# GroupNorm and attention on one core: scalar operands for GpSimd's high parts, and a new order of its list

## The chip, the core and the metric

The kernel runs on one core of a Trainium2 chip. The metric is the device time of one execution in microseconds (us). The profiler records one execution; its span runs from the first to the last recorded instruction. Engines are named as in the profile: PE is TensorE's matmuls and PEld its weight loads, DVE is VectorE, ACT is ScalarE, POOL is GpSimd, SP is SyncE, which here only issues transfers.

## The reference

Eight images `x[b]` of 128 channels by 1024 positions (32 by 32) go through a GroupNorm of 32 groups, a single-head self-attention over the positions, and a residual sum:

```python
h = group_norm(x, gn_w, gn_b)                       # 32 groups of 4 channels
q = einsum('bcn,oc->bno', h, wq) + bq
k = einsum('bcn,oc->bon', h, wk) + bk
v = einsum('bcn,oc->bno', h, wv) + bv
alpha = softmax(q @ k / sqrt(128))                  # 1024 x 1024 for each image
out = einsum('bnc,oc->bon', alpha @ v, wo) + bo
return out + x
```

## The kernel before

The weights are folded once: `wu` stands for wq and wk together, `wvc` for wv and wo together with one column more. For an image (a "batch" `b`, 0 to 7) the kernel makes `h` from x with a scale `ga` and an offset `gc` per channel, `u` from h (what the logits take instead of q), and `v` from h, whose last column gives the bias `c_tok` of each row of logits. To keep float32 accuracy on float16 matmuls, every operand is split in a high part (the value rounded to float16) and a low part (value minus high part), and each product is three matmuls.

The 1024 rows of logits of a batch are 8 tiles of 128. For tile `n`: PE makes the logits in one of three PSUM buffers `S` (lines 537 to 541, `logits`), DVE adds `c_tok` and takes the row extreme (L855, `row_max`), ACT makes the exponentials (L722) and the float16 high part (L733), DVE the low part (L871), SP issues a DMA that transposes both (L234), and PE multiplies by v nine tiles later (`values`, L564 to L566, `LAG = 9`), four tiles at a time into one PSUM bank `O`. All five engines have a list written out by hand, and wait on semaphores. PE's list per batch is: logits of tile n; behind tile 0 the second half of u (`project_u(b, 1)`); behind tiles 1 and 2 the last two parts of v (`project_v`); behind 3 and 5 the first half of u and the first part of v of the next batch; behind 4 and 6 two small matmuls for the statistics of batch b+2; and after each of these one quarter of `values`.

ACT copies u and v out of PSUM to float32 tiles in SBUF (`copy_u` L688, `copy_v` L698) and the products to `av` (`copy_values`, L707). POOL, which cannot reach PSUM, then makes in a round `b` of its list:

- `group_affine(b+1)` (L309 to L318): four instructions of one column that give ga and gc. It waits for the standard deviation.
- `h_parts(b+1, half)`: h (L330), its high part (L333) and its low part (L336), 512 columns each. Half 0 waits until all logits of batch b-1 are done, because the buffer is shared.
- `u_parts(b, 1)` and `u_parts(b+1, 0)`: high and low part of u (L344, L347). The logits of tile 4 of b wait for the first, those of tile 0 of b+1 for the second.
- `row_bias(b, part)` (L355): c_tok of three or two tiles. `row_max` waits for part 0, 1, 2 before tile 0, 3, 6.
- `v_parts(b, part)` (L366, L369): high and low part of v, in parts of 3, 3 and 2 tiles of 128 columns.
- `residual(b)` (L373): adds the output bias to x in place.
- `result(b, q)` (L382, L387): half a batch of the product times the inverse row sums `inv_rows`, plus x. The inverse sums come back over DRAM, spread to all partitions by a DMA that SP issues behind the transpose of tile 2 of the next batch (L221). SP stores a batch when both halves are done.

The order of one round is `group_affine(b+1)`, `h_parts(b+1, 0)`, `u_parts(b, 1)`, `row_bias(b, 1)`, `h_parts(b+1, 1)`, `row_bias(b, 2)`, `v_parts(b, 1)`, `v_parts(b, 2)`, `result(b-2, 1)`, `residual(b)`, `u_parts(b+1, 0)`, `row_bias(b+1, 0)`, `v_parts(b+1, 0)`, `result(b-1, 0)`. Of batch 0 the h and half the u are made by other engines. The high parts are made as a sum with a zero: `zero[:, :].to_broadcast(...)` for h and u, a tensor `zeros` of 3 x 128 columns for v.

The last two tiles are transposed by PE, and the second half of the last batch is finished by DVE (L957, L961).

Of the kernel before, what the change touches and what calls it, by code (L numbers as in the profile page):

```python
# [5 lines left out]
def groupnorm_attention_kernel(  # L6
# [14 lines left out]
    fp32, fp16 = mybir.dt.float32, mybir.dt.float16  # L21
    ALU = mybir.AluOpType
    ACT = mybir.ActivationFunctionType

    B, C, HH, WW = x.shape
    N = HH * WW
# [7 lines left out]
    HALF = 512  # L34
# [12 lines left out]
    with ctx:  # L47
        def sb(name, shape, dt):
            return ctx.enter_context(nc.sbuf_tensor(name, shape, dt))
# [19 lines left out]
        obias = sb("obias", [C, 1], fp32)  # L69

        x_sb = sb("x_sb", [C, B, N], fp32)
# [9 lines left out]
        ga, gc = sb("ga", [C, 2], fp32), sb("gc", [C, 2], fp32)  # L81
        h = sb("h", [C, N], fp32)
        zero = sb("zero", [128, 1], fp32)
        zeros = sb("zeros", [128, 3, C], fp32)
        h_hi, h_lo = sb("h_hi", [C, 2, N], fp16), sb("h_lo", [C, 2, N], fp16)
        u = sb("u", [C, N], fp32)
        v = sb("v", [128, TILES, VW], fp32)
        u_hi, u_lo = sb("u_hi", [C, 2, N], fp16), sb("u_lo", [C, 2, N], fp16)
        v_hi, v_lo = sb("v_hi", [128, 3, TILES, C], fp16), sb("v_lo", [128, 3, TILES, C], fp16)
# [189 lines left out]
        def _(eng):  # L279
# [2 lines left out]
            nc.gpsimd.memset(neg_mean_mat[:, :], -1.0 / GC).then_inc(pool_step, 1)  # L282
            nc.gpsimd.memset(mean_mat[:, :], 1.0 / GC).then_inc(pool_step, 1)
            nc.gpsimd.memset(zero[:, :], 0.0).then_inc(pool_step, 1)
            nc.gpsimd.memset(zeros[:, :, :], 0.0).then_inc(pool_step, 1)
            eng.wait_ge(pool_step, 5)
            nc.gpsimd.affine_select(out=ident[:, :], in_=ident[:, :], compare_op=ALU.not_equal, fill=1.0,
                                    base=0, pattern=[[-1, 128]], channel_multiplier=1).then_inc(consts, 1)
            for m in (neg_mean_mat, mean_mat):
# [4 lines left out]
            eng.wait_ge(consts, 1)  # L294
            nc.gpsimd.tensor_tensor(ident16[:, :], ident[:, :], zero[:, :].to_broadcast([128, 128]),
                                    ALU.add).then_inc(ident_ready, 1)
            eng.wait_ge(pool_step, 7)
            for m in (neg_mean_mat, mean_mat):

                nc.gpsimd.affine_select(out=m[:, :], in_=m[:, :], compare_op=ALU.is_ge, fill=0.0,  # L300
# [20 lines left out]
            def h_parts(b, half):  # L321
                p = b % 2
                cols = slice(half * HALF, (half + 1) * HALF)
                if half == 0:

                    eng.wait_ge(pool_affine, 4 * b)
                    if b >= 2:

                        eng.wait_ge(qk_done, (b - 1) * TILES)
                nc.gpsimd.tensor_scalar(h[:, cols], x_sb[:, b, cols], ga[:, p:p + 1], gc[:, p:p + 1],  # L330
                                        ALU.mult, ALU.add).then_inc(h_made, 1)
                eng.wait_ge(h_made, 2 * b - 1 + half)
                nc.gpsimd.tensor_tensor(h_hi[:, p, cols], h[:, cols], zero[:, :].to_broadcast([C, HALF]),  # L333
                                        ALU.add).then_inc(h_step, 1)
                eng.wait_ge(h_step, 2 * b - 1 + half)
                nc.gpsimd.tensor_tensor(h_lo[:, p, cols], h[:, cols], h_hi[:, p, cols],  # L336
                                        ALU.subtract).then_inc(h_ready, 1)

            def u_parts(b, half):
                p = b % 2  # L340
                cols = slice(half * HALF, (half + 1) * HALF)

                eng.wait_ge(u_out, 2 * b + half)
                nc.gpsimd.tensor_tensor(u_hi[:, p, cols], u[:, cols], zero[:, :].to_broadcast([C, HALF]),  # L344
                                        ALU.add).then_inc(u_step, 1)
                eng.wait_ge(u_step, 2 * b + half)
                nc.gpsimd.tensor_tensor(u_lo[:, p, cols], u[:, cols], u_hi[:, p, cols],  # L347
                                        ALU.subtract).then_inc(u_done, 1)

            def row_bias(b, part):  # L350
                p = b % 2
                t0, n = V_PARTS[part]

                eng.wait_ge(v_out, NV * b + part + 1)
                nc.gpsimd.tensor_tensor(c_tok[:, p, t0:t0 + n], v[:, t0:t0 + n, C],  # L355
                                        cb[:, :].to_broadcast([128, n]), ALU.add).then_inc(c_done, 1)

            def v_parts(b, part):
                r = b % 3
                t0, n = V_PARTS[part]  # L360

                eng.wait_ge(v_out, NV * b + part + 1)
                if part == 0 and b >= 3:

                    eng.wait_ge(av_done, TILES * (b - 2))
                nc.gpsimd.tensor_tensor(v_hi[:, r, t0:t0 + n, :], v[:, t0:t0 + n, 0:C],  # L366
                                        zeros[:, 0:n, :], ALU.add).then_inc(v_step, 1)
                eng.wait_ge(v_step, NV * b + part + 1)
                nc.gpsimd.tensor_tensor(v_lo[:, r, t0:t0 + n, :], v[:, t0:t0 + n, 0:C],  # L369
                                        v_hi[:, r, t0:t0 + n, :], ALU.subtract).then_inc(v_done, 1)  # L370

            def residual(b):
                nc.gpsimd.tensor_tensor(x_sb[:, b, :], x_sb[:, b, :], obias[:, :].to_broadcast([C, N]),  # L373
                                        ALU.add).then_inc(xres_done, 1)

            def result(b, q):

                g = 2 * b + q

                eng.wait_ge(rows_in[b % 2], 16 * (b // 2) + 16)  # L380
                eng.wait_ge(av_out, g + 1)
                nc.gpsimd.tensor_tensor(by_tile(attn[:, q, :]), by_tile(av[:, q, :]), inverses(b, q),  # L382
                                        ALU.mult).then_inc(attn_done, 1)

                eng.wait_ge(xres_done, b + 1)
                eng.wait_ge(attn_done, g + 1)
                nc.gpsimd.tensor_tensor(x_sb[:, b, q * GN:(q + 1) * GN], attn[:, q, :],  # L387
                                        x_sb[:, b, q * GN:(q + 1) * GN], ALU.add).then_inc(y_done, 1)
# [12 lines left out]
            for b in range(B):  # L401
                if b >= 1 and b + 1 < B:
                    group_affine(b + 1)
                    h_parts(b + 1, 0)
                u_parts(b, 1)
                row_bias(b, 1)
                if b + 1 < B:
                    h_parts(b + 1, 1)
                row_bias(b, 2)
                if b == 0:  # L410
                    v_parts(0, 0)
                    u_parts(1, 0)

                    eng.wait_ge(ob_out, 1)
                v_parts(b, 1)
                v_parts(b, 2)
                if b >= 2:
                    result(b - 2, 1)
                residual(b)
                if b + 1 < B:  # L420
                    if b >= 1:
                        u_parts(b + 1, 0)
                    row_bias(b + 1, 0)
                    v_parts(b + 1, 0)
                if b >= 1:
                    result(b - 1, 0)
            result(B - 2, 1)


# [559 lines left out]
```

## Time and profile before

| | |
|---|---|
| device time, three runs | 226.86, 227.68, 227.97 us; median 227.68 |
| device time of the profiled execution | 226.84 us |
| span of the profiled execution | 225.1 us |
| busy: PE, DVE, ACT, POOL | 204.3, 180.7, 176.6, 182.7 us |
| granted clock of PE | 1.00 of full speed |

The profiled execution lasts 1.74 us longer than its span, which is what lies around the recorded instructions. A busy time is a sum over the whole span, and the stages differ, so it does not tell which engine sets the pace of a stage: the rows below are taken batch by batch.

### The profile page before, as it was taken

How to read it: one execution, taken by the hardware profiler on the slowest of the kernel's cores; microseconds unless marked ns; L12 is line 12 of the kernel's file. 1: busy time of each engine (PE TensorE's matmuls, PEld its weight loads, DVE VectorE, ACT ScalarE, POOL GpSimd, SP SyncE). 2: the span in 40 equal slices, each digit the busy share in tenths (PEclk: the TensorE clock that was granted, in tenths of full speed). 3: DMA queues.
4: the chain of work that ended last, by engine and by line, in shares of the span. 5: the costliest groups of instructions: out<-in, count | busy, mean ns of one | idle time of the engine just before them, and what ended most of it. 6: DMA issues, size and time to landing. Idle time of an engine off the chain costs nothing.

```text
span 225.1 us, 3541 instructions
## 1 busy us (share of the span) xinstructions
PE 204.3 (91%) x1137; PEld 105.2 (47%) x1137; DVE 180.7 (80%) x276; ACT 176.6 (78%) x276; POOL 182.7 (81%) x224
## 2 busy tenths in 40 slices
PE   1898667999999999999998989898999979989993
PEld 0764232545454545454543535354544435434763
DVE  1678999999988998988889878798669877887342
ACT  2349989988999799888987889798887879788410
POOL 6039999999899998999999998999999997944500
PEclk9999999999999999999999999999999999999999
DMA  5790999999999899999999999999999999999911
GB/s 160 246 380 7 190 151 191 210 190 217 207 212 184 212 218 213 230 175 230 187 250 169 219 221 202 224 170 241 213 217 184 216 230 153 250 196 238 287 69 52
DMA packets 135314, 45.09 MB, mean 200 GB/s; under 512 B 131328, under 2 KB 132096, under 8 KB 135296
## 3 DMA queue, kind: packets, MB, share of 16 engines
q1 hardware_dynamic: 134720, 44.61, 100.0%
q10 hardware_dynamic: 576, 0.26, 0.4%
q8 instruction: 9, 0.15, 0.3%
q14 instruction: 9, 0.07, 0.1%
HBM read 8.13 MB, written 4.22 MB: 55 GB/s over the span
## 4 chain that ended last, share of the span: by engine, by line
POOL 47%; PE 30%; issue 8%; DVE 6%; DMA 4%; SPq 1%; ACT 1%; POOLq 0%; ACTq 0%
POOL h_lo L336 5%; POOL v_hi L366 5%; POOL v_lo L369 5%; POOL h_hi L333 5%; POOL attn L382 5%; POOL u_lo L347 5%; POOL u_hi L344 4%; PE O L564 4%; POOL x_sb L387 4%; PE O L565 4%; PE O L566 4%; POOL h L330 3%; POOL x_sb L373 3%; PE S L537 3%; PE S L541 3%
## 5 line engine op out<-in xcount | busy, mean ns | idle before, releaser
L855 DVE TENSOR_SCALAR_CACHE_REDUCE neg_logits<-S,c_tok 128x1024 f32<-128x1024 f32 x64 | 81.8, 1278 | 23.6 <-PE S L541 19.2
L722 ACT ACTIVATE S<-neg_logits,exp_bias 128x1024 f32<-128x1024 f32 x64 | 71.6, 1119 | 19.9 <-DVE neg_logits L855 18.7
L871 DVE SCALAR_TENSOR_TENSOR parts<-S,parts 128x1024 f16<-128x1024 f32 x64 | 78.1, 1220 | 2.0 <-ACT parts L733 1.8
L733 ACT ACTIVATE parts<-S 128x1024 f16<-128x1024 f32 x64 | 65.4, 1022 | 1.6
L564 PE MATMUL O<-pT,v_hi 128*128 128x512 f16 x120 | 45.4, 379 | 1.2 <-ACT av L707 1.2
L566 PE MATMUL O<-pT,v_lo 128*128 128x512 f16 x120 | 45.5, 379 | 0.0
L565 PE MATMUL O<-pT,v_hi 128*128 128x512 f16 x120 | 45.5, 379 | 0.0
L537 PE MATMUL S<-h_hi,u_hi 128*128 128x512 f16 x128 | 38.1, 379 | 6.3 <-DVE parts L871 3.7
L541 PE MATMUL S<-h_hi,u_lo 128*128 128x512 f16 x128 | 38.1, 379 | 0.0
L539 PE MATMUL S<-h_lo,u_hi 128*128 128x512 f16 x128 | 38.1, 379 | 0.0
L382 POOL TENSOR_TENSOR attn<-av,inv_rows 128x512 f32<-128x512 f32 x14 | 21.3, 1523 | 6.6 <-DMA inv_rows<-inv_line 6.2
L537 PEld LDWEIGHTS S<-h_hi,u_hi 128*128 128x128 f16 x128 | 11.9, 99 | 21.8 <-issue 7.2
L369 POOL TENSOR_TENSOR v_lo<-v,v_hi 128x384 f16<-128x384 f32 (+1 forms) x24 | 19.4, 807 | 1.9
L366 POOL TENSOR_TENSOR v_hi<-v,zeros 128x384 f16<-128x384 f32 (+1 forms) x24 | 20.4, 848 | 0.0
L541 PEld LDWEIGHTS S<-h_hi,u_lo 128*128 128x128 f16 x128 | 12.5, 98 | 15.1
L539 PEld LDWEIGHTS S<-h_lo,u_hi 128*128 128x128 f16 x128 | 12.5, 98 | 15.1
L387 POOL TENSOR_TENSOR x_sb<-attn,x_sb 128x512 f32<-128x512 f32 x14 | 17.8, 1268 | 2.0
L566 PEld LDWEIGHTS O<-pT,v_lo 128*128 128x128 f16 x120 | 11.7, 98 | 14.2
L347 POOL TENSOR_TENSOR u_lo<-u,u_hi 128x512 f16<-128x512 f32 x15 | 17.4, 1157 | 1.2
L564 PEld LDWEIGHTS O<-pT,v_hi 128*128 128x128 f16 x120 | 12.5, 104 | 12.2 <-issue 1.8
L336 POOL TENSOR_TENSOR h_lo<-h,h_hi 128x512 f16<-128x512 f32 x14 | 16.2, 1156 | 1.1
L565 PEld LDWEIGHTS O<-pT,v_hi 128*128 128x128 f16 x120 | 11.7, 97 | 10.3
(137 smaller groups left out, 294.2 us busy)
## 6 DMA issues: line engine op xcount, KB each, us to landing
x_sb<-in_x_dram SPq DMA_DIRECT2D x7, 512.0 KB, 8.4
inv_rows<-inv_line SPq DMA_DIRECT2D x7, 512.0 KB, 4.8
out_dram<-x_sb SPq DMA_DIRECT2D x6, 512.0 KB, 3.7
pT<-parts SPq DMA_TRANSPOSE x62, 4.9
out_dram<-x_sb SPq DMA_DIRECT2D x3, 256.0 KB, 3.6
x_sb<-in_x_dram SPq DMA_DIRECT2D x2, 256.0 KB, 3.9
out_dram<-x_sb SPq DMA_DIRECT2D x2, 128.0 KB, 1.9
inv_line<-row_inv SPq DMA_DIRECT2D x7, 4.0 KB, 2.5
```

What stands on the lines that cost most here:

```text
L366: nc.gpsimd.tensor_tensor(v_hi[:, r, t0:t0 + n, :], v[:, t0:t0 + n, 0:C], zeros[:, 0:n, :], ALU.add).then_inc(v_step, 1)
L382: nc.gpsimd.tensor_tensor(by_tile(attn[:, q, :]), by_tile(av[:, q, :]), inverses(b, q), ALU.mult).then_inc(attn_done, 1)
L537: nc.tensor.matmul(s[:, c], q_hi, h_hi[:, p, c], start=True, stop=False)
L539: nc.tensor.matmul(s[:, c], q_hi, h_lo[:, p, c], start=False, stop=False)
L541: last = nc.tensor.matmul(s[:, c], q_lo, h_hi[:, p, c], start=False, stop=True)
L564: nc.tensor.matmul(O[:, :], vh, ph, start=(m == 0), stop=False)
L565: nc.tensor.matmul(O[:, :], vh, pl, start=False, stop=False)
L566: last = nc.tensor.matmul(O[:, :], vl, ph, start=False, stop=(m == TILES - 1))
L722: nc.scalar.activation(S[T % 3][:, :], neg_logits[:, n % 2, :], ACT.Exp, scale=-1.0, bias=exp_bias[:, p, n:n + 1], accum_out=row_sum[:, p, ...
L733: nc.scalar.activation(parts[:, T % SPLITS, 0:N], S[T % 3][:, :], ACT.Copy, scale=P_SCALE).then_inc(hi_done, 1)
L855: nc.vector.tensor_scalar(neg_logits[:, n % 2, :], S[T % 3][:, :], c_tok[:, p, n:n + 1], None, ALU.add, ALU.min, accum_out=exp_bias[:, p, ...
L871: nc.vector.scalar_tensor_tensor(out=parts[:, T % SPLITS, N:2 * N], in0=S[T % 3][:, :], scalar=P_SCALE, in1=parts[:, T % SPLITS, 0:N], op0 ...
```

## The change

The high parts of u and v are made by `tensor_scalar` with two immediate scalars (times 1.0, plus 0.0) in place of `tensor_tensor` with a zero. The high part of h is made from x with ga and gc as per-partition scalars, as h itself is, and no longer from h. The residual takes the output bias as a per-partition scalar and an immediate 0.0. The tensor `zeros` and its memset go. In POOL's list `row_bias(b, 1)` goes ahead of `u_parts(b, 1)`; `result(b-2, 1)` and `u_parts(b+1, 0)` go ahead of `v_parts(b, 1)` and `v_parts(b, 2)`; `residual(b)` goes to the end of the round, behind `result(b-1, 0)`.

```diff
-        zeros = sb("zeros", [128, 3, C], fp32)
...
-            nc.gpsimd.memset(zeros[:, :, :], 0.0).then_inc(pool_step, 1)
-            eng.wait_ge(pool_step, 5)
+            eng.wait_ge(pool_step, 4)
...
-            eng.wait_ge(pool_step, 7)
+            eng.wait_ge(pool_step, 6)
...
-                nc.gpsimd.tensor_tensor(h_hi[:, p, cols], h[:, cols], zero[:, :].to_broadcast([C, HALF]),
-                                        ALU.add).then_inc(h_step, 1)
+                nc.gpsimd.tensor_scalar(h_hi[:, p, cols], x_sb[:, b, cols], ga[:, p:p + 1], gc[:, p:p + 1],
+                                        ALU.mult, ALU.add).then_inc(h_step, 1)
...
-                nc.gpsimd.tensor_tensor(u_hi[:, p, cols], u[:, cols], zero[:, :].to_broadcast([C, HALF]),
-                                        ALU.add).then_inc(u_step, 1)
+                nc.gpsimd.tensor_scalar(u_hi[:, p, cols], u[:, cols], 1.0, 0.0,
+                                        ALU.mult, ALU.add).then_inc(u_step, 1)
...
-                nc.gpsimd.tensor_tensor(v_hi[:, r, t0:t0 + n, :], v[:, t0:t0 + n, 0:C],
-                                        zeros[:, 0:n, :], ALU.add).then_inc(v_step, 1)
+                nc.gpsimd.tensor_scalar(v_hi[:, r, t0:t0 + n, :], v[:, t0:t0 + n, 0:C], 1.0, 0.0,
+                                        ALU.mult, ALU.add).then_inc(v_step, 1)
...
-                nc.gpsimd.tensor_tensor(x_sb[:, b, :], x_sb[:, b, :], obias[:, :].to_broadcast([C, N]),
-                                        ALU.add).then_inc(xres_done, 1)
+                nc.gpsimd.tensor_scalar(x_sb[:, b, :], x_sb[:, b, :], obias[:, :], 0.0,
+                                        ALU.add, ALU.add).then_inc(xres_done, 1)
...
+                row_bias(b, 1)
                 u_parts(b, 1)
-                row_bias(b, 1)
                 if b + 1 < B:
                     h_parts(b + 1, 1)
                 row_bias(b, 2)
...
+                if b >= 2:
+                    result(b - 2, 1)
+                if b >= 1 and b + 1 < B:
+                    u_parts(b + 1, 0)
                 v_parts(b, 1)
                 v_parts(b, 2)
-                if b >= 2:
-                    result(b - 2, 1)
-                residual(b)
                 if b + 1 < B:
-                    if b >= 1:
-                        u_parts(b + 1, 0)
                     row_bias(b + 1, 0)
                     v_parts(b + 1, 0)
                 if b >= 1:
                     result(b - 1, 0)
+                residual(b)
             result(B - 2, 1)
```

## Rows read from the trace of the kernel before

**Rows 1.** Windows: edges, length; busy of PE, PEld, DVE, ACT, POOL; granted clock.
```profile
39.45:107.85 68.40, 68.39 (x376) 33.85 (x377) 62.86 (x95) 61.51 (x96) 64.76 (x76) 1.00 1.14 208
...
84.04:107.85 23.81, 23.81 (x131) 11.78 (x130) 21.39 (x33) 21.26 (x33) 22.42 (x28) 1.00 1.13 212
107.85:133.26 25.41, 24.07 (x131) 11.64 (x130) 21.13 (x32) 22.12 (x34) 24.02 (x29) 1.00 1.11 209
...
158.70:184.14 25.44, 23.69 (x127) 11.27 (x126) 19.53 (x25) 21.28 (x32) 24.05 (x29) 1.00 1.13 212
```

**Rows 2.** Timeline of POOL, first instruction of two successive rounds: start us, us.
```profile
85.69 0.34 POOL L309 TENSOR_SCALAR newton<-var_eps,rstd 128x1 f32<-128x1 f32 x1
...
111.13 0.34 POOL L309 TENSOR_SCALAR newton<-var_eps,rstd 128x1 f32<-128x1 f32 x1
```

**Rows 3.** Timeline of POOL, DVE, PE, batches 4 to 6; brackets: idle before.
```profile
118.05 0.20 POOL L355 TENSOR_TENSOR c_tok<-v,cb 128x3 f32<-128x3 f32 x1
118.35 1.28 DVE L855 TENSOR_SCALAR_CACHE_REDUCE neg_logits<-S,c_tok 128x1024 f32<-128x1024 f32 x1 [1.14 <-issue]
...
130.51 1.16 POOL L347 TENSOR_TENSOR u_lo<-u,u_hi 128x512 f16<-128x512 f32 x1
131.77 0.59 PE L537 MATMUL S<-h_hi,u_hi 128*128 128x512 f16 x2 [0.70 <-issue]
...
174.78 0.38 PE L564 MATMUL O<-pT,v_hi 128*128 128x512 f16 x1 [0.51 <-ACT av L707]
```

**Rows 4.** Groups of POOL by line and shape: busy us, mean ns, idle before.
```profile
L344 POOL TENSOR_TENSOR u_hi<-u,zero 128x512 f16<-128x512 f32 x15 | 15.6, 1038 | 0.0
L366 POOL TENSOR_TENSOR v_hi<-v,zeros 128x384 f16<-128x384 f32 x16 | 15.3, 954 | 0.0
L373 POOL TENSOR_TENSOR x_sb<-x_sb,obias 128x1024 f32<-128x1024 f32 x8 | 15.1, 1893 | 0.0
L333 POOL TENSOR_TENSOR h_hi<-h,zero 128x512 f16<-128x512 f32 x14 | 14.5, 1039 | 1.2
...
L330 POOL TENSOR_SCALAR h<-x_sb,ga,gc 128x512 f32<-128x512 f32 x14 | 10.7, 767 | 0.7
L366 POOL TENSOR_TENSOR v_hi<-v,zeros 128x256 f16<-128x256 f32 x8 | 5.1, 636 | 0.0
...
L318 POOL TENSOR_SCALAR gc<-neg_mean,ga,gb 128x1 f32<-128x1 f32 x7 | 2.4, 341 | 0.7
...
L312 POOL TENSOR_SCALAR newton<-newton 128x1 f32<-128x1 f32 x7 | 1.3, 191 | 0.6
```

**Rows 5.** Timeline of SP, POOL, ACT, DVE and PE, batches 2 and 3.
```profile
75.78 0.59 SPq L221 DMA_DIRECT2D inv_rows<-inv_line  x1
...
82.75 1.54 POOL L382 TENSOR_TENSOR attn<-av,inv_rows 128x512 f32<-128x512 f32 x1
...
87.29 0.77 POOL L330 TENSOR_SCALAR h<-x_sb,ga,gc 128x512 f32<-128x512 f32 x1
...
88.05 0.50 ACT L698 COPY v<-M 128x387 f32<-128x387 f32 x1
...
90.37 1.04 POOL L344 TENSOR_TENSOR u_hi<-u,zero 128x512 f16<-128x512 f32 x1
...
93.32 1.27 DVE L855 TENSOR_SCALAR_CACHE_REDUCE neg_logits<-S,c_tok 128x1024 f32<-128x1024 f32 x1
...
95.05 0.59 PE L537 MATMUL S<-h_hi,u_hi 128*128 128x512 f16 x2
```

**Rows 6.** L221's instructions: time to landing; DMA issues by line, median us to landing.
```profile
DMA to landing us min/median/max: 4.2/4.8/5.6
...
x_sb<-in_x_dram SPq DMA_DIRECT2D x7, 512.0 KB, 8.4
```

**Rows 7.** Timeline of the tail, POOL and DVE.
```profile
205.63 1.52 POOL L382 TENSOR_TENSOR attn<-av,inv_rows 128x512 f32<-128x512 f32 x1 [6.17 <-DMA inv_rows<-inv_line]
...
216.59 0.69 DVE L957 SCALAR_TENSOR_TENSOR attn_last<-O,inv_rows 128x512 f32<-128x512 f32 x1 [2.00 <-PE O L566]
```

## The prediction

> **What bounds the kernel now.** I read the windows first, cut at the first row_max of each batch, because shares over the whole span mix stages. In batches 1 to 3 TensorE has no gap at all: 68.39 us busy in 68.40, and a batch takes 23.81 us [rows 1]. That is the pace of TensorE with its list full; DVE and ACT are near 21.3 us in the same windows, so neither is close to it. Batches 4, 5 and 6 take 25.41, 25.44 and 25.44 us (5 is like 6 in length and like 4 in its work) with the same list on TensorE. Something else sets the pace there.
>
> The timeline of POOL says what. Its rounds begin at 85.69 and 111.13, 25.44 us apart, already while TensorE needs 23.81 [rows 2, 1]. Inside a round its instructions stand back to back; the wait of 0.0 in the groups of u_hi, v_hi and the residual says the same [rows 4]. So GpSimd is full from batch 2 on and falls behind by 25.44 - 23.81 = 1.63 us a round. For two rounds that eats a lead; from batch 4 on it is a wait. The timeline shows where: the c_tok of tiles 3 to 5 begins at 118.05 and lasts 0.20, and the row_max that needs it starts at 118.35, after 1.14 us of idle DVE; u_lo for the next batch ends at 130.51 + 1.16 = 131.67, and the logits that need it start at 131.77, after 0.70 us of idle TensorE [rows 3]. The profile calls both "issue", since it links no semaphore to them; the times link them. Batches 0 and 1 are no case of this: GpSimd is late in nothing there, and I expect nothing from them.
>
> **The change part by part.** The high part of h costs 1039 ns and becomes the very instruction that makes h, 767 ns; only the output type differs [rows 4]. That type looks free: the biased residual (1024 columns, float32 out) and u_hi (512 columns, float16 out), both a sum with a broadcast, differ by 855 ns for 512 columns, 1.67 ns each, and that slope leaves the same 0.18 us of fixed time that a tiny instruction has. Two per round save 2 x 272 = 0.54 us.
>
> For u, v and the residual no row shows the new form at size. From 341 ns for one column with two pointer scalars (L318) to 767 ns for 512 (L330) the slope is 426 / 511 = 0.834 ns a column; with two immediates one column costs 191 ns (L312) [rows 4]. So u_hi: 191 + 426 = 617 ns instead of 1038, saving 2 x 421 = 0.84. v_hi: 510 instead of 954 and 404 instead of 636, saving 2 x 444 + 232 = 1.12. The residual, with one pointer, lies between the two fixed costs: 266 + 853 = 1119 instead of 1893, saving 0.77. Sum 0.54 + 0.84 + 1.12 + 0.77 = 3.27 us a round, and a round of 25.44 - 3.27 = 22.17. The bound on the other side is the slope of the broadcast sums, 1.67 ns: then u, v and the residual save nothing. I take the slope of L330, the nearest row: same opcode, same engine, one input tensor.
>
> What is late next is TensorE. A round has to lose only 1.63 of the 3.27 us before TensorE's 23.81 governs, so all beyond that is hidden under matmuls and buys nothing.
>
> The Trainium skill (GPSIMD Engine Reference, section 3.1, the cycle accounting of elementwise work) puts the best loop with one input at about 1.8 cycles an element, 768 ns for 512. The 767 ns of L330 agree, but the 341 ns for one column do not: by that rule the whole 767 would be loop. By its slope the savings would be 0.54 for h, 0.54 for u, 1.01 for v and 0.36 for the residual, an estimate of 2.45 us, and a round of 23.0: still under TensorE, with 0.8 us to spare instead of 1.6.
>
> The new order. c_tok of tiles 3 to 5 now goes ahead of u of the second half, so POOL's list can stand at it until ACT has copied that v, while u, the second half of h and all behind them queue. In batch 3 the copy ends at 88.55 [rows 5]. How late does GpSimd get there? Its last work of the round before is the result that waits for the inverse row sums: their DMA is issued at 75.78 [rows 5] and lands at most 5.6 us later [rows 6], 81.38. Result and affine then take 87.29 - 82.75 = 4.54 [rows 5], the residual, now in between, 1.12, the first half of h 90.37 - 87.29 - 0.27 = 2.81 [rows 5], c_tok 0.20: 90.05. So the copy is long there; row_max of tile 3 wants c_tok at 93.32 [rows 5], 3.3 us later. u follows with 0.62 + 0.08 + 1.16 = 1.86, ends at 91.9, and the logits of tile 4 want it at 95.05 [rows 5]: 3.1 us to spare. The edit costs nothing while these covers stand. The two parts of v go behind a result and a u, 2.9 + 1.9 = 4.8 us later; the products that read them run a batch later, and ACT's next copy over them too. The u for the next batch comes earlier, which helps. Moving the residual adds 1.12 us ahead of the next affine (counted above). In the tail the last residual waits behind the result that starts at 205.63, ends near 205.63 + 2.94 + 1.12 = 209.7, and DVE asks for it at 216.59 [rows 7]. SP's stores come behind the results in the same order. The memset that goes ran before any data was there: nothing.
>
> **The sum.** Batch 4: 25.41 - 23.81 = 1.60. Batch 5: 25.44 - 23.81 = 1.63. Batch 6 has no statistics to make, 24.07 - 23.69 = 0.38 us less TensorE work than batch 4 [rows 1], so its floor is 23.43; but the wait of 0.51 us for ACT's copy of the product [rows 3] may stay, 23.94. I take 23.7 and a gain of 1.74. Together 4.97. The profiled execution took 226.84 us (span 225.1 and 1.74 around it): 226.84 - 4.97 = 221.87. The three runs lie 0.0 to 1.1 us above it, the median 0.84. I add 0.5 and forecast 222.4 us. What a measurement can tell from no change is some 0.5%, 1.1 us.
>
> **The rivals.**
>
> *Only the order pays (chance 0.07).* If float16 output or the strided v keep the new forms at the old slope, a round stays near 25.4. For it: no row shows the forms at size. Against: the output type is free in the broadcast sums. Then c_tok is in time, and the second half of u ends 0.2 us later than now, near 118.25 in batch 4; TensorE wants it at 95.05 + 23.81 = 118.86, so batch 4 is whole, batch 5 loses 118.25 + 25.44 - 118.86 - 23.81 = 1.02 and batch 6 the full 1.63. 2.65 of 4.97 remain, a gain of 2.3: 226.84 - 2.3 + 0.5 = 225.0.
>
> *GpSimd was not the cause (0.03).* Another thing that slows batches 4 to 6, a growing queue of transposes say, would leave 227.3. Against it stands the fit of two waits to ends on POOL within 0.1 us [rows 3].
>
> *The inverse row sums come later (0.05), and the kernel is slower.* Their DMA shares its queue with the transposes, and with the residual behind the result a late landing now delays the residual, the affine, h, c_tok and u in a row. For it: loads of 512 KB took 8.4 us to land [rows 6], the same size. Against: these seven never took over 5.6. It decides from 5.6 + 3.1 = 8.7 us on; each us beyond costs a us in each of five batches (3 to 7). At 10.3 us: 5 x 1.6 = 8.0 lost, 4.97 won, 226.84 + 3.0 + 0.5 = 230.3.
>
> **How the numbers follow.** Forecast as argued 0.82 (its own range 221.0 to 223.6: batch 6 either way, the run 0 to 1.1 above the sum, a lost half us in covers); the rivals as given; 0.03 for a gain above 6 us, of a kind that I do not see. The range runs from 220.9 to 225.2, which takes in the first rival. Faster 0.82 + 0.07 + 0.03 = 0.92, same 0.03, slower 0.05.
>
> **What would show it.** Windows of batches 4 and 5 of 23.8 us with TensorE full; u_hi near 620 ns, v_hi near 510 and 400, h_hi 767, the residual near 1120; gaps on POOL of 1.5 us or so a round, ended by the DMA of the inverse sums or ACT's copies; no idle DVE ahead of tile 3. It is wrong if POOL still stands back to back with 25 us rounds, if the new forms cost over 0.8 us, or if TensorE waits ahead of tile 3 or 4 in batches that are full now.

## The result, and the profile after

| | before | changed |
|---|---|---|
| median of 22 runs each | 226.79 us | 226.63 us |
| lowest to highest | 225.83 to 227.99 | 223.74 to 228.15 |
| profiled execution, span | 226.84, 225.1 us | 224.92, 223.2 us |

The ratio to the kernel before is 0.9933, 95% interval 0.9907 to 0.9958. Here and below a ratio leaves out executions that took over 1.5% more than the fastest of their kernel, here six of the changed kernel and none of the kernel before. Over all 22 the medians differ by 0.16 us and the means by 0.8. By this measurement the change wins at most 0.7%, about 1.5 us, where 2% were forecast, and the median lies above the range. A second measurement of the changed kernel, below, gave 0.9901 (0.9866 to 0.9937), median 224.67 us.

The groups of POOL in the changed kernel, which answer to [rows 4] (line numbers are two lower), show three forms where they were expected and one that was not:

```profile
L371 POOL TENSOR_SCALAR x_sb<-x_sb,obias 128x1024 f32<-128x1024 f32 x8 | 29.6, 3703 | 0.0
...
L331 POOL TENSOR_SCALAR h_hi<-x_sb,ga,gc 128x512 f16<-128x512 f32 x14 | 10.8, 772 | 1.4
L342 POOL TENSOR_SCALAR u_hi<-u 128x512 f16<-128x512 f32 x15 | 9.3, 622 | 0.6 <-ACT u L686 0.6
L364 POOL TENSOR_SCALAR v_hi<-v 128x384 f16<-128x384 f32 x16 | 8.2, 515 | 0.0
...
L364 POOL TENSOR_SCALAR v_hi<-v 128x256 f16<-128x256 f32 x8 | 3.3, 408 | 0.0
```

The high parts came within 6 ns of 767, 617, 510 and 404. The residual takes 3703 ns, not 1119; it was 1893. The timeline of POOL has the rounds of batches 4 and 5:

```profile
113.04 0.34 POOL L307 TENSOR_SCALAR newton<-var_eps,rstd 128x1 f32<-128x1 f32 x1
...
134.33 3.71 POOL L371 TENSOR_SCALAR x_sb<-x_sb,obias 128x1024 f32<-128x1024 f32 x1
138.02 0.35 POOL L307 TENSOR_SCALAR newton<-var_eps,rstd 128x1 f32<-128x1 f32 x1
```

138.02 - 113.04 = 24.98 us a round, instead of 25.44 before [rows 2] and 22.17 forecast: GpSimd still sets the pace. The windows, cut at the first row_max of batches 3, 4, 5 and 6 as in [rows 1], say so too:

```profile
83.67:107.82 24.15, 23.80 (x131) 11.68 (x130) 22.31 (x32) 21.27 (x33) 22.84 (x28) 1.00 1.11 213
107.82:132.80 24.98, 23.97 (x131) 11.60 (x130) 22.44 (x32) 21.25 (x33) 23.53 (x29) 1.00 1.11 205
132.80:157.77 24.97, 23.96 (x131) 11.60 (x130) 22.44 (x32) 21.24 (x33) 23.52 (x29) 1.00 1.10 214
157.77:182.24 24.47, 23.70 (x127) 11.24 (x126) 19.63 (x25) 20.85 (x31) 23.01 (x29) 1.00 1.13 212
```

Batches 4 to 6 win 0.43, 0.47 and 0.97 us instead of 1.60, 1.63 and 1.74. Batch 3, full before, loses 0.34. The timeline of PE, DVE and POOL shows what waits now:

```profile
97.53 1.52 POOL L380 TENSOR_TENSOR attn<-av,inv_rows 128x512 f32<-128x512 f32 x1
97.63 1.43 DVE L814 SCALAR_TENSOR_TENSOR spread<-dmean,mv 128x1 f32<-128x1 f32 x1
99.21 0.22 PE L431 MATMUL M<-wvc_hi,h_hi 128*128 128x129 f16 x1 [0.35 <-DVE spread L814]
...
117.68 0.38 PE L431 MATMUL M<-h_hi,wu_hi 128*128 128x512 f16 x1 [0.62 <-POOL h_lo L334]
117.80 1.28 DVE L853 TENSOR_SCALAR_CACHE_REDUCE neg_logits<-S,c_tok 128x1024 f32<-128x1024 f32 x1 [0.61 <-issue]
```

At 117.68 TensorE waits for GpSimd's first half of h, and DVE for c_tok at 117.80, in place of the waits of [rows 3]: GpSimd is late, at another point of its round. At 97.63 DVE's one-column instruction for the statistics of batch 5 takes 1.43 us, and ends at 99.06 when GpSimd's long multiplication ends at 99.05; TensorE then waits 0.35 us for it. That is the whole 0.34 of batch 3. In batches 4 and 5 the same wait, 0.38 us each time, comes on top of the one for h:

```profile
124.18 0.22 PE L431 MATMUL M<-wvc_hi,h_hi 128*128 128x129 f16 x1 [0.38 <-DVE spread L814]
```

Whether it comes in batch 3 is a matter of tenths: in the profile of the second measurement DVE's instruction takes 1.07 us there, TensorE does not wait for it, and batch 3 keeps its 23.80 us.

### The profile page after: what moved, and what is told of

It reads as the page before. It is cut to its first block, busy times and chain, and to the rows that moved or that the text cites. A ratio compares the mean times of both kernels' runs of the same rounds, so it can differ in the third digit from the quotient of the medians.

```text
span 223.2 us, 3540 instructions
## 1 busy us (share of the span) xinstructions
PE 204.1 (91%) x1137; PEld 105.2 (47%) x1137; DVE 182.9 (82%) x276; ACT 175.9 (79%) x276; POOL 179.1 (80%) x223
## 4 chain that ended last, share of the span: by engine, by line
PE 74%; DVE 9%; issue 5%; ACT 4%; POOL 4%; DMA 2%; ACTq 0%; POOLq 0%
PE O L562 10%; PE O L563 10%; PE O L564 10%; PE S L539 9%; PE S L535 9%; PE S L537 9%; DVE neg_logits L853 5%; PE M L431 3%; PE M L433 3%; PE M L432 3%; DVE spread L814 2%; ACT S L720 2%; DMA wk_sb<-in_L_conv_wk_dram 2%; POOL h_lo L334 2%; ACT parts L731 1%
## 5 line engine op out<-in xcount | busy, mean ns | idle before, releaser
L720 ACT ACTIVATE S<-neg_logits,exp_bias 128x1024 f32<-128x1024 f32 x64 | 71.6, 1119 | 18.5 <-DVE neg_logits L853 17.3
L371 POOL TENSOR_SCALAR x_sb<-x_sb,obias 128x1024 f32<-128x1024 f32 x8 | 29.6, 3703 | 0.0
L539 PEld LDWEIGHTS S<-h_hi,u_lo 128*128 128x128 f16 x128 | 12.5, 98 | 15.1
L537 PEld LDWEIGHTS S<-h_lo,u_hi 128*128 128x128 f16 x128 | 12.5, 98 | 15.1
L562 PEld LDWEIGHTS O<-pT,v_hi 128*128 128x128 f16 x120 | 12.5, 105 | 11.8 <-issue 1.4
```

The source lines that it names most:

```text
L371: nc.gpsimd.tensor_scalar(x_sb[:, b, :], x_sb[:, b, :], obias[:, :], 0.0, ALU.add, ALU.add).then_inc(xres_done, 1)
L537: nc.tensor.matmul(s[:, c], q_hi, h_lo[:, p, c], start=False, stop=False)
L539: last = nc.tensor.matmul(s[:, c], q_lo, h_hi[:, p, c], start=False, stop=True)
L562: nc.tensor.matmul(O[:, :], vh, ph, start=(m == 0), stop=False)
L720: nc.scalar.activation(S[T % 3][:, :], neg_logits[:, n % 2, :], ACT.Exp, scale=-1.0, bias=exp_bias[:, p, n:n + 1], accum_out=row_sum[:, p, ...
```

## The experiments

Each run's ratio is to the kernel before on the same chip.

**Which forms are slow.** Behind the last result of the changed kernel GpSimd runs thirteen more instructions, each waiting for the one before (the waits are left out here), with `flat` for the 1024 columns of attn:

```diff
             result(B - 2, 1)
+            eng.wait_ge(y_done, 2 * B - 2)
+            nc.gpsimd.tensor_scalar(flat, h, obias, 0.0, ALU.add, ALU.add)      # L429
+            nc.gpsimd.tensor_scalar(h, h, obias, 0.0, ALU.add, ALU.add)         # L431
+            nc.gpsimd.tensor_scalar(flat, h, 0.5, 0.0, ALU.add, ALU.add)        # L433
+            nc.gpsimd.tensor_scalar(flat, h, obias, obias, ALU.add, ALU.add)    # L435
+            nc.gpsimd.tensor_scalar(flat, h, 1.0, obias, ALU.mult, ALU.add)     # L437
+            nc.gpsimd.tensor_scalar(h, h, 1.0, obias, ALU.mult, ALU.add)        # L439
+            nc.gpsimd.tensor_scalar(flat, h, obias, obias, ALU.mult, ALU.add)   # L441
+            nc.gpsimd.tensor_scalar(flat, h, obias, None, ALU.add)              # L443
+            nc.gpsimd.tensor_scalar(flat, h, obias, 1.0, ALU.add, ALU.mult)     # L445
+            nc.gpsimd.tensor_scalar(flat, h, obias, 1.0, ALU.mult, ALU.mult)    # L447
+            nc.gpsimd.tensor_scalar(attn[:, 0, :], h[:, 0:HALF], obias, 0.0, ALU.add, ALU.add)  # L449
+            nc.gpsimd.tensor_scalar(f16_out, h, obias, 0.0, ALU.add, ALU.add)   # L451
+            nc.gpsimd.tensor_scalar(flat, h, 1.0, 0.0, ALU.mult, ALU.add)       # L453
```

> The changed kernel, and behind its last result GpSimd runs thirteen more instructions on scratch tiles, one after another, each waiting for the one before; the total time says nothing, their durations do. The biased residual measured 3.70 us in the changed kernel where 1.12 was forecast. Theory A, the pair of operations: add followed by add is slow in itself. Then every add-add form of 1024 columns takes about 3.7 us, in place or not, with a pointer, two pointers or two immediates, float32 or float16 out, 512 columns about 1.9 to 2.0, and mult-add with the same operands about 1.1 us, in place or not. Theory B, in place: forms that write where they read take 3.7 us, also as mult-add, and add-add into another tile about 1.1. Theory C, a pointer mixed with an immediate: add-add with two pointers or two immediates about 1.1, mult-add with an immediate and a pointer 3.7. Theory D, the width: all of 1024 columns are slow and the one of 512 takes 0.7 to 0.8.

The timeline of POOL in that run, start and duration in us (L429, L435, L447 and L453 took 3.71, 3.78, 1.12 and 1.05):

```profile
218.26 3.71 POOL L431 TENSOR_SCALAR h<-h,obias 128x1024 f32<-128x1024 f32 x1
222.06 3.63 POOL L433 TENSOR_SCALAR attn<-h 128x1024 f32<-128x1024 f32 x1
...
229.68 1.12 POOL L437 TENSOR_SCALAR attn<-h,obias 128x1024 f32<-128x1024 f32 x1
230.90 1.12 POOL L439 TENSOR_SCALAR h<-h,obias 128x1024 f32<-128x1024 f32 x1
...
233.43 2.85 POOL L443 TENSOR_SCALAR attn<-h,obias 128x1024 f32<-128x1024 f32 x1
236.38 1.12 POOL L445 TENSOR_SCALAR attn<-h,obias 128x1024 f32<-128x1024 f32 x1
...
238.81 2.01 POOL L449 TENSOR_SCALAR attn<-h,obias 128x512 f32<-128x512 f32 x1
240.91 3.71 POOL L451 TENSOR_SCALAR f_out<-h,obias 128x1024 f16<-128x1024 f32 x1
```

Theory A. Add-add is slow in every dress: in place or not, immediates or pointers, float32 or float16 out, and at half the width. With a product for one of the two adds, or for both, the same instruction takes 1.05 to 1.20 us. Mixed operands, the in-place write and the width are out. Add alone, for which the expectation has no figure, takes 2.85.

A second list asked how far that goes. It has the same frame and, in this order, L429 to L453 (in brackets the two scalars and the operations):

```diff
+ (0.5, None, add)  (obias, None, mult)  (obias, None, subtract)  (1.0, obias, mult, subtract)
+ (obias, 1.0, subtract, mult)  (obias, 0.0, subtract, subtract)  (obias, None, max)
+ (1.0, 0.0, mult, max)  (0.0, 0.0, add, max)  tensor_copy to float32  tensor_copy to float16
+ tensor_tensor with obias broadcast, add  (0.5, 0.0, add, add)
```

> As the first run with forms behind the last result, thirteen others on the same scratch tiles, 1024 columns each; only their durations count. In the first run add-add took 3.6 to 3.8 us with any operands and add alone 2.85, while mult-add, add-mult and mult-mult took 1.05 to 1.2. Theory P, a product anywhere in the instruction makes it fast: mult alone, mult-subtract, subtract-mult and mult-max take about 1.1 us, add alone, subtract alone, subtract-subtract and add-max 2.8 to 3.8. Theory Q, only pairs of two operations with mult or add are special and all else is slow: mult alone, mult-subtract, subtract-mult and mult-max take 2.8 us or more. The copies are 1.0 to 1.1 us or 2.8 by either; the sum with a broadcast tensor stays at 1.9, add-add with two immediates at 3.6.

```profile
215.97 2.85 POOL L431 TENSOR_SCALAR attn<-h,obias 128x1024 f32<-128x1024 f32 x1
...
221.87 3.71 POOL L435 TENSOR_SCALAR attn<-h,obias 128x1024 f32<-128x1024 f32 x1
225.68 3.71 POOL L437 TENSOR_SCALAR attn<-h,obias 128x1024 f32<-128x1024 f32 x1
...
236.22 3.64 POOL L443 TENSOR_SCALAR attn<-h 128x1024 f32<-128x1024 f32 x1
...
244.74 1.04 POOL L449 CAST f_out<-h 128x1024 f16<-128x1024 f32 x1
245.86 1.89 POOL L451 TENSOR_TENSOR attn<-h,obias 128x1024 f32<-128x1024 f32 x1
```

Theory Q. A single operation, mult too (L431), takes 2.8 to 2.9 us; mult-subtract, subtract-mult and mult-max 3.6 to 3.7, as add-add. Fast, of what was tried, are the three pairs of mult and add with at least one mult, and the copies.

**The residual put right.** First by the old sum of two tensors, then as a product with 1.0 and a sum:

```diff
-                nc.gpsimd.tensor_scalar(x_sb[:, b, :], x_sb[:, b, :], obias[:, :], 0.0,
-                                        ALU.add, ALU.add).then_inc(xres_done, 1)
+                nc.gpsimd.tensor_tensor(x_sb[:, b, :], x_sb[:, b, :], obias[:, :].to_broadcast([C, N]),
+                                        ALU.add).then_inc(xres_done, 1)
```

> The changed kernel with the residual alone put back to the sum of two tensors (1.89 us). Theory: the slow residual is what held the gain back. A round of GpSimd is then 24.98 - 1.81 = 23.2 us, under TensorE's 23.81; batches 4 and 5 take 23.8 us with TensorE full, and the time is 3 to 4 us below the changed kernel, about 222 us on the profiled execution. Rival: TensorE, DVE or the transposes hold batches 4 to 6 near 25 us whatever GpSimd does; then the time stays within 1 us of the changed kernel.

```diff
-                nc.gpsimd.tensor_scalar(x_sb[:, b, :], x_sb[:, b, :], obias[:, :], 0.0,
-                                        ALU.add, ALU.add).then_inc(xres_done, 1)
+                nc.gpsimd.tensor_scalar(x_sb[:, b, :], x_sb[:, b, :], 1.0, obias[:, :],
+                                        ALU.mult, ALU.add).then_inc(xres_done, 1)
```

> The changed kernel with the residual as x times 1.0 plus the bias, mult and add in place of add and add, everything else the same. Theory A (the pair of operations): 1.1 to 1.2 us for the residual, a GpSimd round of 24.98 - 2.58 = 22.4 us, batches 4 and 5 at 23.8 us, and the same time as with the sum of two tensors within 0.5 us, since both rounds are under TensorE's. Theories B, C and D (in place, mixed operands, width): the residual stays at 3.7 us and the time at that of the changed kernel.

Medians 224.53 and 224.35 us, ratios 0.9851 (0.9815 to 0.9887) and 0.9886 (0.9836 to 0.9937); the profiled executions took 222.09 and 224.42. The intervals overlap: the two are not told apart, as forecast. The profiled execution of the first has the 222 us that were expected, but by the ratios it wins 1.1 to 1.9 us over the changed kernel and not 3 to 4.

The 2.33 us between the two profiled executions are no effect of the residual. 2.22 of them lie ahead of the first row_max, here in the first and then in the second:

```profile
16.00 1.28 DVE L853 TENSOR_SCALAR_CACHE_REDUCE neg_logits<-S,c_tok 128x1024 f32<-128x1024 f32 x1 [0.56 <-PE S L539]
...
18.22 1.28 DVE L853 TENSOR_SCALAR_CACHE_REDUCE neg_logits<-S,c_tok 128x1024 f32<-128x1024 f32 x1 [1.28 <-PE S L539]
```

In the second, TensorE waits 0.93 us at 11.15 for the load of the output bias, in the first it does not. In the fourteen profiles of this document that start lasts between 15.5 and 18.2 us, so profiles are compared from the first row_max on: 208.7 us to the end of the span in the kernel before, 206.8 in the changed kernel, 204.3 and 204.5 in these two.

The residual's group in the second:

```profile
L371 POOL TENSOR_SCALAR x_sb<-x_sb,obias 128x1024 f32<-128x1024 f32 x8 | 9.0, 1122 | 0.0
```

Windows of the first, batches 3, 6 and the rest from batch 7's first row_max on:

```profile
83.26:107.06 23.80, 23.80 (x131) 11.80 (x130) 21.22 (x32) 21.17 (x33) 20.81 (x28) 1.00 1.12 211
...
154.67:178.34 23.67, 23.54 (x127) 11.36 (x126) 19.62 (x26) 20.88 (x31) 20.86 (x28) 1.00 1.10 209
178.34:220.30 41.96, 36.75 (x234) 20.91 (x232) 25.52 (x35) 24.38 (x34) 19.27 (x18) 1.00 0.98 198
```

Batches 4 and 5 are like 3, in both versions. That is the floor of TensorE which the prediction named, with the 23.7 for batch 6. But the stretch from batch 7 on, 40.96 us before and after the change, is 1.0 us longer. The timeline of PE has the reason, and that of SP its history:

```profile
205.46 0.38 PE L562 MATMUL O<-pT,v_hi 128*128 128x512 f16 x1 [0.89 <-DMA pT<-parts]
```

```profile
45.06 1.02 SPq L211 DMA_DIRECT2D inv_line<-row_inv  x1
...
193.44 0.53 SPq L211 DMA_DIRECT2D inv_line<-row_inv  x1
```

TensorE waits for a transpose. SP issues the write of the inverse sums behind the transpose of tile 0 of each batch. In batch 1 that is 8.4 us after the first row_max (36.68), in batch 7 15.1 us after it (178.34): (193.44 - 45.06) / 6 = 24.73 us a batch. The queue of transposes is slower than TensorE's 23.8; nine tiles of lag hide it until the tail. The trace of the kernel before had the sign already: there the same write goes from 8.8 us behind the first row_max in batch 1 (37.45) to 11.8 in batch 4 (107.85), (119.64 - 46.25) / 3 = 24.46 us a batch, before the batches themselves grow to 25.4:

```profile
46.25 0.78 SPq L212 DMA_DIRECT2D inv_line<-row_inv  x1
...
119.64 0.53 SPq L212 DMA_DIRECT2D inv_line<-row_inv  x1
```

**Where the queue is full.** The five stores inside the loop were issued by ACT instead of SP; then they were left out.

```diff
-                    if n == 7 and 2 <= b < B - 1:
-                        eng.wait_ge(y_done, 2 * b - 2)
-                        store(b - 2, slice(0, N))
...
                     high_part(b, n)
+                    if n == 7 and 2 <= b < B - 1:
+                        act.wait_ge(y_done, 2 * b - 2)
+                        act.dma_start(out_d[b - 2, :, :], x_sb[:, b - 2, :]).then_inc(y_out, 16)
```

> The new order with the residual as mult and add, and the five stores of whole batches inside the loop issued by ACT instead of SP. With a batch every 23.8 us the write of the inverse sums, which SP issues behind the transpose of tile 0, slips from 8.7 us after the first row_max in batch 1 to 15.1 in batch 7, and in the tail TensorE waits 0.9 us for a transpose. Theory A: SP's issuing is what is slow, the slip shrinks to 12 us or less and the wait in the tail goes; about 0.9 us less. Theory B: the DMA engines are what is full, the bytes are the same, the slip and the wait stay.

Median 224.72, ratio 0.9892 (0.9853 to 0.9931). The write still comes 15.3 us behind in batch 7, and TensorE waits for transposes three times, first in batch 6 (0.96 us at 160.71) and then, early in batch 7:

```profile
185.28 0.38 PE L558 MATMUL O<-pT,v_hi 128*128 128x512 f16 x1 [0.74 <-DMA pT<-parts]
```

Without the stores (the same edit without the lines on ACT):

> The same kernel, without the five stores of whole batches inside the loop (batches 0 to 4 are not written; batches 5 to 7 are). Theory A and theory B of the kernel with the stores on ACT both expect the slip to shrink, to 12 us or less in batch 7, and no wait for transposes in the tail, by A because SP issues less, by B because 2.5 MB less pass the DMA engines. If the slip stays near 15 us, neither the issuing of the stores nor their bytes matter, and the transposes alone are slower than 23.8 us a batch.

Median 221.63, ratio 0.9765 (0.9731 to 0.9799). SP's last write of inverse sums, and the window of the tail, of which the first edge is batch 7's first row_max:

```profile
187.41 0.53 SPq L211 DMA_DIRECT2D inv_line<-row_inv  x1
```

```profile
178.27:219.10 40.83, 36.60 (x234) 20.86 (x232) 25.52 (x35) 24.37 (x34) 13.95 (x15) 1.00 0.83 165
```

187.41 - 178.27 = 9.1 us: no slip, no wait for a transpose, the tail back at its length. So for the stores it is what passes through the DMA engines and not who issues it: theory B. What holds the transposes themselves stays open. SP's issue of one lasts 2.5 us in the median of the version with the sum of two tensors (the row has lowest, median and highest in ns), 20 us for the eight of a batch:

```profile
L233 SPq DMA_TRANSPOSE pT<-parts x62: 1316/2529/4783, 20.9 to 205.6; - x62
```

That SP could issue them no faster, whatever the DMA engines do, is a rival that no run tests.

**A version that beats both.** The residual as mult and add, and the stores of batches 3 and 4 behind the loop:

```diff
-                    if n == 7 and 2 <= b < B - 1:
+                    if n == 7 and 2 <= b < B - 3:
...
-            eng.wait_ge(y_done, 2 * B - 4)
-            store(B - 3, slice(0, N))
+            for late in (B - 5, B - 4, B - 3):
+                eng.wait_ge(y_done, 2 * late + 2)
+                store(late, slice(0, N))
```

> The new order with the residual as mult and add, and the stores of batches 3 and 4 moved behind the loop, so that 1.0 MB less pass the DMA engines between the transposes of batches 5 to 7. Without any of the five stores the slip of the inverse sums' write stayed at 9.1 us in batch 7 and nothing waited in the tail. Theory (the DMA engines are full at 23.8 us a batch): the slip in batch 7 falls from 15.1 to 12 or 13 us, the tail's wait of 0.9 us goes, and the time falls by 0.5 to 1.0 us if the late stores end before the last rows do. Rival: they do not, and the last stores land later by more than what is won.

Median 221.42 us, ratio 0.9774 (0.9744 to 0.9805), runs from 220.63 to 222.37. The last write, against the first row_max of batch 7 at 178.40, is 12.6 us behind, and no wait for a transpose is left:

```profile
191.01 1.09 SPq L211 DMA_DIRECT2D inv_line<-row_inv  x1
```

On the same chip the version with stores in the loop and the changed kernel ran again.

> The new order with the residual as mult and add once more, now beside the changed kernel on the same chip. Theory: 23.8 us a batch from batch 2 to 6, and a ratio to the kernel before of 0.985 to 0.99, below that of the changed kernel by 0.5 to 1%. If the two have the same ratio, the slow residual does not cost what the traces say.

> The changed kernel itself, beside the versions of this call. Theory: GpSimd's rounds of 24.98 us, a ratio to the kernel before of 0.991 to 0.996 as measured first.

0.9853 (0.9811 to 0.9894), median 224.07, against 0.9901 (0.9866 to 0.9937), median 224.67. The direction is as expected, but the intervals overlap; the windows are what tells them apart, here batch 5 of the one and then of the other:

```profile
132.40:156.20 23.80, 23.80 (x131) 11.80 (x130) 21.62 (x32) 21.26 (x33) 20.82 (x28) 1.00 1.13 219
...
132.71:157.63 24.92, 23.97 (x131) 11.61 (x130) 22.43 (x33) 21.23 (x33) 23.46 (x29) 1.00 1.11 214
```

Against the version with the stores in the loop, the late stores win 2.65 us in the median, more than the 0.5 to 1.0 expected, and the mechanism accounts for little of it. The spans of the two profiles differ by 2.3 us, and 1.96 of that is the start. Behind it the tail is 0.83 us shorter, and batch 5 is 0.56 longer: there TensorE waits 0.37 us for DVE's one-column instruction, which takes 1.45 beside GpSimd's multiplication. Why the other executions are as short, no profile shows.

**What the order does.** The new order with all the old instructions:

```diff
-                nc.gpsimd.tensor_scalar(u_hi[:, p, cols], u[:, cols], 1.0, 0.0,
-                                        ALU.mult, ALU.add).then_inc(u_step, 1)
+                nc.gpsimd.tensor_tensor(u_hi[:, p, cols], u[:, cols], zero[:, :].to_broadcast([C, HALF]),
+                                        ALU.add).then_inc(u_step, 1)
...
```

> The new order of GpSimd's list with all the old instructions (sums with zeros, the tensor of zeros back). The rounds of GpSimd stay at 25.4 us. By the first rival of the prediction c_tok is in time, batch 4 is whole at 23.8 us, batch 5 loses about 1.0 us and batch 6 1.6: 2.3 us less than the kernel before. If instead the residual behind the result, or c_tok ahead of u, costs as much as it gives, the time is that of the kernel before within 0.5 us.

Median 226.88, ratio 0.9987 (0.9955 to 1.002): nothing that can be told from no change. In the profile batches 4 and 5 are 24.57 and 25.49 us; the first rival of the prediction had 23.8 and 24.8:

```profile
107.70:132.27 24.57, 24.14 (x131) 11.65 (x130) 21.24 (x32) 21.15 (x33) 23.18 (x28) 1.00 1.09 210
132.27:157.76 25.49, 24.14 (x131) 11.64 (x130) 21.25 (x33) 21.14 (x33) 24.10 (x29) 1.00 1.09 204
```

TensorE waits there at 117.16 (0.24 us) and 142.65 for the first half of h:

```profile
142.65 0.38 PE L433 MATMUL M<-h_hi,wu_hi 128*128 128x512 f16 x1 [1.15 <-POOL h_lo L336]
```

The u of the next batch, behind tile 3, needs it, and the residual now stands in front of it. The prediction did not list that deadline. The old order with the forms of the change, and then with the residual as mult and add too:

```diff
-                row_bias(b, 1)
                 u_parts(b, 1)
+                row_bias(b, 1)
...
                 v_parts(b, 1)
                 v_parts(b, 2)
+                if b >= 2:
+                    result(b - 2, 1)
+                residual(b)
...
-                residual(b)
             result(B - 2, 1)
```

> The old order with the scalar forms as the change has them, the residual as add and add (3.70 us), ahead of u for the next batch. The round is 24.98 us as in the changed kernel, so batches 4 to 6 take 25.0 us from the first one that is late. Theory: in steady state the round's sum counts and not the order, so the time is that of the changed kernel plus at most one round's loss, 0 to 1.5 us more. Rival: with u behind the long residual, each batch's first logits wait further and the time is above that of the kernel before.

Median 223.77, ratio 0.9878 (0.9837 to 0.9919). Its windows, batches 5 and 6:

```profile
132.94:157.64 24.70, 23.97 (x131) 11.71 (x130) 21.15 (x33) 22.04 (x34) 23.24 (x29) 1.00 1.10 215
157.64:182.58 24.94, 23.70 (x127) 11.27 (x126) 19.63 (x26) 21.23 (x32) 23.48 (x30) 1.00 1.12 213
```

The rival is out, and the time is not even above that of the changed kernel: from the first row_max on the two profiles take 205.6 and 206.8 us.

> The old order of GpSimd's list with all the scalar forms, the residual as mult and add (1.12 us). A round of GpSimd is 22.4 us, under TensorE's 23.81. Theory: with GpSimd under TensorE the order is worth nothing; batches 3 to 5 take 23.8 us and the time is that of the new order with the same residual within 0.5 us. Rival: the order is needed, since c_tok and u are late in the round even when the round is short; then row_max of tile 3 still waits and the batches stay above 24.3 us.

Median 226.34, ratio 0.9907 (0.9867 to 0.9947); the twelve runs lie between 223.02 and 228.85, and the profiled one took 227.11 us. Batches 2 to 6 take 23.8 to 23.9 us there, as the theory has it, and then PE's timeline and two windows behind it have

```profile
208.82 0.47 PE L562 MATMUL O<-pT,v_hi 128*128 128x512 f16 x1 [2.79 <-DMA pT<-parts]
```

```profile
208.80:222.50 13.70, 13.16 (x88) 8.24 (x88) 3.37 (x7) 1.01 (x1) 3.69 (x3) 0.88 0.76 168
...
210.00:212.00 2.00, 2.00 (x6) 0.68 (x5) 0.00 (x0) 0.00 (x0) 1.86 (x2) 0.50 1.74 107
```

a wait of 2.79 us for a transpose, and a mean granted clock of 0.88 in the stretch after it: TensorE, idle before, runs part of it at 0.50, 1.2 GHz instead of 2.4. By the ratios no pair of versions shows the new order to be worth anything: with add-add the old one is as good or better, with mult-add they are not told apart. Over all twelve runs, though, the old order with mult-add is at 226.34 against 226.80 us for the kernel before, where the new one wins 2.5 to 2.9 us in the median; that the order is worth something there is not ruled out.

## Why the prediction was wrong

**What bounds the kernel: right.** GpSimd sets the pace of batches 4 to 6 and TensorE's 23.8 us is the floor under it. With the residual put right all of batches 2 to 6 stand on that floor, 23.67 in batch 6 where 23.7 was taken.

**The sum: one term, and it decides.** The step that failed is "I take the slope of L330, the nearest row: same opcode, same engine, one input tensor". For u and v that held, because the change gives them L330's pair of operations, mult and add. The residual has add and add, and no row of before shows that pair at any width. Forecast to save 0.77 us a round, it cost 1.81 more. The other three saved 0.53 + 0.83 + 1.11 = 2.47, so the round should have been 25.44 - 2.47 + 1.81 = 24.78; 24.98 was measured, and the 0.2 us more are not traced. "A round has to lose only 1.63" was the right test, and the round lost 0.46. That "POOL still stands back to back with 25 us rounds" was the prediction's own sign of being wrong. The bound from the other side, the slope of the broadcast sums at 1.67 ns, was no bound: add-add has (3.71 - 2.01) us / 512 = 3.32 ns a column. The fall to no saving at all was a rival; a loss was not, since no row was slower than those sums.

The Trainium skill (GPSIMD Engine Reference, section 7, performance pitfalls) names 4 cycles an element for a dependent chain of float32 operations, an estimate of 3.33 ns at the 1.2 GHz that it gives for this engine. The measured 3.32 ns has that size; that the slow form is such a chain no run shows.

**The order: its cover was miscounted.** "The edit costs nothing while these covers stand" listed c_tok and u, not the first half of h for the u of the next batch, and not what GpSimd's longer instructions do to DVE. In batches 3 to 5 of the changed kernel the result that was moved ahead runs while DVE makes its statistics, which costs 0.34 to 0.38 us each; that the move is to blame is not shown, since the old order with the same instructions has one such wait too, 0.42 us in its batch 4. The Trainium skill says that a DVE instruction with two SBUF inputs and a GpSimd one that reads SBUF exclude each other for a whole instruction (SBUF — State Buffer, Who interferes with whom); the two ends at 99.06 and 99.05 agree, and the prediction should have weighed it. One pair does not agree: in the old order with add-add, DVE's instruction is as short as alone in the middle of the residual, which reads SBUF too:

```profile
49.56 3.70 POOL L371 TENSOR_SCALAR x_sb<-x_sb,obias 128x1024 f32<-128x1024 f32 x1
51.27 0.22 DVE L814 SCALAR_TENSOR_TENSOR spread<-dmean,mv 128x1 f32<-128x1 f32 x1
```

**The rivals.** The first came nearest in the profile (a gain of 2.3 us, 1.92 measured), but by luck: the high parts did get cheap, and the batches that it had whole and late are not those of the trace. The third did not come: the inverse sums land as before (median 4.5 us, 4.8 before). The queue of transposes, thrown out with the second rival, is the next bound: not the cause in batches 4 to 6 of the kernel before, but with GpSimd out of the way it takes back 1.0 us in the tail. So even with the residual at 1.12 us the forecast 4.97 would have been too much by about that: from the first row_max on the two profiles of that version win 4.2 and 4.5 us. The ratios 0.9886 and 0.9853 are only 2.6 to 3.3 us of 227; the start, which varies, may hold the difference, but no profile shows that.

**What stays open.** Why the runs of the changed kernel spread over 4.4 us, the kernel before over 2.2. The start, which spread over 2.7 us in the profiles, is one candidate. The two kernels with less in the DMA queue spread over 0.9 and 1.7 us, and one long execution shows a wait for a transpose and a fall of the clock behind it. The listed clocks bear that out for the versions with a short residual and SP's stores in the loop: 13 of their 36 runs have a mean granted clock of 0.992 and took 225.06 to 228.88 us, the other 23, with 0.997 to 1.00, 222.09 to 226.59. The changed kernel's long runs are not of this kind: all its 28 runs have 0.997 to 1.00.

## What to carry to other kernels

Price a new instruction from a row with the same operations, not only the same opcode and shape; where none exists, run that one instruction behind the kernel's last step and read its duration before anything is argued from it. Compare two profiles from the same step of the program on, and not by their spans, when the start varies. When one engine is about to stop being the bound, look for queues that just keep up with it (here by how far SP's fixed step slips behind its batch), because they take the pace next and give part of the gain back late. List every reader of what a list makes before reordering it, the small ones on other engines too.

## What the runs showed of the hardware

- GpSimd's `tensor_scalar` on 1024 float32 columns: 1.05 to 1.20 us for mult-add, add-mult and mult-mult; 2.78 to 2.85 for a single add, mult, subtract or max; 3.6 to 3.8 for add-add, subtract-subtract, mult-subtract, subtract-mult, mult-max and add-max. Copies take 1.04, to float16 too; a sum with a broadcast column 1.89.
- A one-column DVE instruction with its inputs in SBUF, 0.22 us alone, took 1.43 beside a GpSimd instruction of 1.52 us, and ended with it. Beside the add-add residual of 3.70 us it took 0.22.
- The DMA queue here carries a batch of eight transposes with one 512 KB store and the spreading of the inverse sums in about 24.7 us (all loads of x are issued in the first 9 us); issuing the stores from another engine does not help, and without their 2.5 MB the queue keeps step with batches of 23.8.
- After a wait of 2.79 us idle, TensorE's mean granted clock over the next 13.7 us was 0.88 of 2.4 GHz, some of it at 1.2.
